# A selective scan fed by a conditioner: group loads two transfers a step, and two chains of small steps placed sooner on TensorE, ScalarE and VectorE

## The reference

```python
def _L0_cond_ref(x, ...):                      # the conditioner
    ctx = causal_ema(x, tau_ctx)
    wg = sigmoid(concat([x, ctx]) @ Wg.T + bg)
    gated = x * wg
    h1 = gelu(x @ Wn1.T + bn1)
    mod = 0.5 + sigmoid(h1 @ Wn2.T + bn2)      # one factor for each token and each of 8 traces
    traces = [causal_ema(gated * mod[d], tau[d]) for d in range(8)]
    temporal = sum(traces[d] * softmax(blend)[d] for d in range(8))
    gate = sigmoid(temporal @ Wtemp.T + btemp)
    soma = gelu(x @ Wsoma.T + bsoma)
    out = (soma * gate) @ Wout.T
    return (out - mean(out)) / sqrt(var(out) + 1e-5) * gamma + beta

def _L0_attn_ref(y, ...):                      # the mixer: a selective scan with 16 states, 512 channels
    xc, z = split(y @ W_in.T)
    xc = silu(causal_conv4(xc))
    dt, B, C = split(xc @ W_x.T)
    delta = softplus(dt @ W_dt.T + b_dt)
    for t: h = exp(delta[t] * A) * h + delta[t] * B[t] * xc[t];  y[t] = C[t] . h + D * xc[t]
    return (y * silu(z)) @ W_out.T
```

## Time and profile before

| | before |
|---|---|
| time, median of 3 runs | 3850.71 us (3850.57 to 3854.19) |
| the profiled execution | 3854.34 us |
| its span in the trace | 3852.6 us |
| granted TensorE clock, mean | 0.915 of full speed |
| busy: PE, DVE, ACT, POOL | 84%, 56%, 42%, 16% of the span |
| the stretch of the scans, 170 to 1640 us | DVE busy 1266.8 of 1470 us |

### The profile page before, as it was taken

The page is one execution under the profiler, slowest core; times in us unless marked ns, Lnnn a source line. Parts: engine busy times, 40 slices in busy tenths (PEclk is TensorE's granted clock), DMA queues, the critical chain, the costliest instruction groups (busy, mean ns, idle before and its releaser), DMA issues. The chain is left out here.

```text
span 3852.6 us, 40852 instructions
## 1 busy us (share of the span) xinstructions
PE 3246.7 (84%) x12812; PEld 1756.5 (46%) x12813; DVE 2152.1 (56%) x2705; ACT 1601.1 (42%) x3089; POOL 625.1 (16%) x767
## 2 busy tenths in 40 slices
PE   7677878787877864279979999999999999987996
PEld 5343434334343421046644444444444444445775
DVE  2398889888888888822223352535353444433334
ACT  3555555555656553123313242423333232322443
POOL 0000201020101010223310020201102020205772
PEclk8898989898888886589989999999999999998998
DMA  1345454636363646441230000000101010036557
GB/s 60 90 113 128 127 135 118 149 106 157 101 156 98 153 120 154 113 157 65 67 130 0 20 35 26 29 29 26 44 11 54 1 54 1 32 131 201 157 155 263
DMA packets 193227, 362.86 MB, mean 94 GB/s; under 512 B 28274, under 2 KB 85106, under 8 KB 191922
## 3 DMA queue, kind: packets, MB, share of 16 engines
q1 hardware_dynamic: 164514, 296.19, 27.2%
q0 software_dynamic: 20352, 57.17, 4.0%
q10 hardware_dynamic: 8208, 7.54, 0.6%
HBM read 250.53 MB, written 110.28 MB: 94 GB/s over the span
## 5 line engine op out<-in xcount | busy, mean ns | idle before, releaser
L1630 DVE TENSOR_TENSOR_SCAN hs<-dA,hs 128x2048 f32<-128x2048 f32 x128 | 566.2, 4423 | 7.0
L449 POOL COPY rows<-slot 128x64 f32<-128x64 f32 x48 | 13.4, 310 | 2796.1 <-DVE new_pl L586 2763.0
L2217 PE MATMUL ps<-pT,V 128*128 128x512 f32 x1024 | 450.7, 593 | 0.9 <-DVE pT L2385 0.9
L1471 ACT ACTIVATE dA<-dl,w_An 128x511 f32<-128x511 f32 x512 | 326.0, 711 | 204.7 <-DVE hs L1630 167.7
L1622 DVE TENSOR_TENSOR hs<-u,bb 128x2048 f32<-128x2048 f32 x128 | 292.6, 2286 | 108.7 <-DMA bb<-bcd 82.5
L1310 PE MATMUL ps<-hs,w_S 128*32 128x512 f32 x1024 | 170.2, 735 | 204.5 <-DVE hs L1636 204.5
L2217 PEld LDWEIGHTS ps<-pT,V 128*128 128x128 f32 x1024 | 189.6, 190 | 221.2 <-issue 214.8
L1636 DVE TENSOR_TENSOR hs<-hs,cb 128x2048 f32<-128x2048 f32 x128 | 289.9, 2266 | 0.0
L1787 POOL DMA_INDIRECT slots<-og,idt x232 | 242.4, 1045 | 260.4 <-DVE og L1875 197.2
L445 POOL DMA_INDIRECT sorted<-rows,new_pl x192 | 259.6, 1352 | 63.6 <-issue 44.8
L2292 ACT ACTIVATE pp<-ps,nm 128x512 f32<-128x512 f32 x256 | 172.6, 686 | 215.2 <-DVE nm L2368 215.2
(11 more groups left out here) (354 smaller groups left out, 5473.3 us busy)
## 6 DMA issues: line engine op xcount, KB each, us to landing
bb<-bcd SPq DMA_DIRECT2D x128, 256.0 KB
cb<-bcd SPq DMA_DIRECT2D x128, 256.0 KB
dl<-dld SPq DMA_DIRECT2D x128, 256.0 KB, 7.1
u<-ud SPq DMA_DIRECT2D x128, 256.0 KB, 9.3
xg<-sorted SPq DMA_DIRECT2D x232, 136.0 KB, 2.1
slots<-zeros SPq DMA_DIRECT2D x136, 128.0 KB, 3.8
qrg<-slots SPq DMA_DIRECT2D x32, 512.0 KB, 16.3
rg<-slots SPq DMA_DIRECT2D x32, 256.0 KB, 4.7
```

Source lines behind the costliest of these rows:

```text
L1471: act.activation(m.dA[:, N % 2, q, 1:T], m.dl[:, G % 2, q, 1:T], ACT.Exp, scale=An[:, e, N % GROUP:N % GROUP + 1]).then_inc(s_da, 1)
L1630: dve.tensor_tensor_scan(state, m.dA[:, N % 2].rearrange("p j t -> p (j t)"), state, 0.0, ALU.mult, ALU.add).then_inc(s_h, 1)
L2217: ins = pe.matmul(ps[:, 6 + j, :], V[:, m, h * D + j * P:h * D + (j + 1) * P], pT[:, i % 2, h % 2, m, :], start=(h == 0 and m == 0), stop= ...
```

## The change

1. **Group loads.** `spread_group` is split into `spread_delta` and `spread_u`. The first group of each subject is still brought in whole in step 14. Each of the other three is brought in over four steps, two transfers a step: delta in the first two, u in the last two. Before, the eight transfers stood in one step (3, 7 and 15).
2. **Conditioner, first pieces.** The product and the scaling of trace 0 of subject b + 2 move from step 0 of the next subject to step 15, `gate_product` over steps 13 and 14, and `gated_ready` from step 15 to step 14. `z_product` is cut in two halves between them.
3. **Conditioner, end.** ScalarE does `copy_ends` and `tempo_ready` ahead of the decays of step 7, and `cond_scale` ahead of those of step 9. TensorE does `cond_out_product` in step 8 and `variance_product` at the head of step 9. VectorE does `soma_gated` between `scan` and `out` of step 8, and `cond_ready` ahead of the gate of step 9.
4. **Delta.** TensorE does `rank_product` ahead of `mod_product` and `delta_product` already in step 12; ScalarE does `rank_ready` ahead of `mod_ready` and of the decays.
5. **Setup.** The table of decays is made from one copy of the identity in place of eight, after the first `gated_ready`; `setup_pe` runs in step 1 in place of 5, `setup_act` in step 4 in place of 5.

```diff
-        def spread_group(sp, m, G):
+        def spread_delta(sp, m, G, ns):
             j = G % JI
             sp.wait_ge(m_st if j else m_st0, 32 * (G // JI + 1))
             if G >= 2:
                 sp.wait_ge(s_da, GROUP * GROUP * (G - 1))
-            for n in range(GROUP):
+            for n in ns:
                 sp.dma_start(m.dl[LINE * n:LINE * (n + 1), G % 2], dld[j].rearrange("(q c) t -> c q t", c=LINE)
                              ).then_inc(s_dl[G % 2], 16)
...
@@ SyncE, in each step
-                            if n in (3, 7):
-                                spread_group(sp, m, JI * b + 2 + n // 4)
-                            if n == 15 and kc is not None:
-                                spread_group(sp, m, JI * kc + 1)
+                            G = (N + 1) // GROUP + 1
+                            if G % JI and 2 <= G < JI * B:
+                                piece = (N + 1) % GROUP
+                                spread = spread_delta if piece < 2 else spread_u
+                                spread(sp, m, G, range(piece % 2 * 2, piece % 2 * 2 + 2))
@@ ScalarE
                         elif n == 7:
-                            decays_ahead()
                             if kc is not None:
                                 copy_ends(act, c, kc)
                                 tempo_ready(act, c, kc)
+                            decays_ahead()
...
                         elif n == 9:
+                            if kc is not None:
+                                cond_scale(act, c, kc)
                             decays_ahead()
-                            if kc is not None:
-                                cond_scale(act, c, kc)
...
                             if kc is not None:
                                 conv_ready(act, m, kc, 3)
+                                rank_ready(act, c, kc)
                             if ke is not None:
                                 mod_ready(act, ke)
                             decays_ahead()
-                            if kc is not None:
-                                rank_ready(act, c, kc)
...
+                        else:
+                            if ke is not None:
+                                scale_turned(act, c, ke, 0, 0)
+                            if b >= 0 and kc is not None:
+                                decays(NS * kc)
+                            if ke is not None:
+                                scale_turned(act, c, ke, 0, 1)
                             decays_ahead()
@@ VectorE
+                            if n == 8 and b + 1 < B:
+                                soma_gated(dve, c, b + 1)
                             if N:
                                 out(N - 1)
...
                         elif n == 9:
+                            if kc is not None:
+                                cond_ready(dve, c, kc)
                             if b >= 0:
                                 gate(b, 1)
-                            if kc is not None:
-                                cond_ready(dve, c, kc)
...
-                        elif n == 15 and ke is not None:
+                        elif n == 14 and ke is not None:
                             gated_ready(dve, c, ke)
@@ VectorE, setup
+                ch.link(dve.tensor_copy(f.decay[:, :, :], ident[:, :].unsqueeze(1).to_broadcast([P, NTR, P])))
                 for d in range(NTR):
-                    ch.link(dve.tensor_copy(f.decay[:, d, :], ident[:, :]))
-                    ch.link(dve.tensor_tensor_scan(f.decay[:, d, :], ...
+                    ch.step(dve.tensor_tensor_scan(f.decay[:, d, :], ...
+                ch.all_but(0)
```

More of the change, by code:

```diff
@@ L301, in setup_dve @@
                 assert ch.n == f.averages, ch.n
-            elif part == 2:
+            elif part == 3:
                 ch.step(dve.tensor_copy(ones_b[:, :], ones[:, :]))
@@ L863, in delta_product, with z_product @@
                 product(pe, ps[:, 4 + j, :], [(Wdt[:, j * P:(j + 1) * P], c.dts)], m_dl)
-        def z_product(pe, k):
+        def z_product(pe, k, js):
             pe.wait_ge(m_pre, JI * (k + 1))
-            for j in range(JI):
+            for j in js:
                 product(pe, ps[:, 4 + j, :], [(Win[:, i, DI + j * P:DI + (j + 1) * P], y[:, i, :]) for i in range(DC)], m_z)
@@ L1250, in _ @@
                     for G in (0, 1):
-                        spread_group(sp, m, G)
+                        spread_delta(sp, m, G, range(GROUP))
+                        spread_u(sp, m, G, range(GROUP))
                     for b in range(B):
@@ L1335, in tasks @@
                             if kc is not None:
-                                turn_gated(pe, c, kc, 0, 0)
-                            if b > 0:
-                                add_state(NS * b - 1)
-                            if kc is not None:
-                                turn_gated(pe, c, kc, 0, 1)
+                                turn_gated(pe, c, kc, 1, 0)
                             if b >= 0:
@@ L1343, in tasks @@
                             if kc is not None:
-                                turn_gated(pe, c, kc, 1, 0)
+                                turn_gated(pe, c, kc, 1, 1)
+                            if b > 0:
+                                add_state(NS * b - 1)
                         elif n == 1:
@@ L1421, in tasks @@
                             convolution(pe, m, kc, 3)
+                            rank_product(pe, m, kc)
                             if ke is not None:
                                 mod_product(pe, c, ke)
-                            rank_product(pe, m, kc)
-                        elif n == 13 and kc is not None:
                             delta_product(pe, c, kc)
+                        elif n == 13 and ke is not None:
+                            gate_product(pe, c, ke, 0)
                         elif n == 14 and ke is not None:
-                            gate_product(pe, c, ke, 0)
                             gate_product(pe, c, ke, 1)
                         elif n == 15 and kc is not None:
-                            z_product(pe, kc)
+                            if ke is not None:
+                                turn_gated(pe, c, ke, 0, 0)
+                            z_product(pe, kc, (0, 1))
+                            if ke is not None:
+                                turn_gated(pe, c, ke, 0, 1)
+                            z_product(pe, kc, (2, 3))
                     pe.wait_ge(masks, MASKS)
@@ L1438, in _ @@
                     gate_product(pe, c, 0, 1)
-                    pe.wait_ge(f.su, f.averages)
+                    pe.wait_ge(f.su, f.mixed)
+                    turn_gated(pe, c, 0, 0, 0)
+                    turn_gated(pe, c, 0, 0, 1)
                     for n in range(NS):
-                        if n == 5:
+                        if n == 1:
                             setup_pe(pe, f)
+                            pe.wait_ge(f.su, f.averages)
                         if n == 8:
@@ L1455, in _ @@
                                 add_state(NS * b + n - 1)
-                            if n == 9 and kc is not None:
-                                variance_product(pe, c, kc)
                     add_state(last - 1)
@@ L1495, in tasks @@
                                 gate_of_z(b)
-                            if kc is not None:
-                                scale_turned(act, c, kc, 1, 0)
                         elif n == 1:
-                            if kc is not None:
-                                scale_turned(act, c, kc, 1, 1)
                             decays_ahead()
@@ L1599, in _ @@
                     gate_ready(act, c, 0, 1)
+                    scale_turned(act, c, 0, 0, 0)
+                    scale_turned(act, c, 0, 0, 1)
                     for n in range(NS):
-                        if n == 5:
+                        if n == 4:
                             setup_act(act, f, 1)
@@ L1663, in tasks @@
                                 route_choice(dve, v, rt, k)
-                        elif n == 8:
+                        elif n == 8 and k is not None:
+                            route_places(dve, v, rt, kc, k)
+                        elif n == 9:
                             if kc is not None:
-                                soma_gated(dve, c, kc)
-                            if k is not None:
-                                route_places(dve, v, rt, kc, k)
-                        elif n == 9:
+                                cond_ready(dve, c, kc)
                             if b >= 0:
                                 gate(b, 1)
-                            if kc is not None:
-                                cond_ready(dve, c, kc)
                         elif n == 11 and ke is not None:
```

45 lines of the change are left out of this document (26 added, 19 removed).

## The result

The changed kernel takes 3789.9 us (median of 4 runs, 3786.0 to 3794.2), the kernel before 3851.7 beside it: ratio 0.984, 95% interval 0.9828 to 0.9852, or 62 us less. The forecast was 3774, 76 us less; the range of 3718 to 3818 holds the result, and so does the own range of case (a).

The account below looks back on a forecast made before the run. VectorE's own work and waits set the scans' time, with 174 us of waits to win. Terms -50, +11, -40, +14, -8.5 and -2.7 sum to -76, taking 3850.7 to 3774 us; range 3718 to 3818.

Parts of the forecast that it names:

- case (a): Whole kernel: the terms add up as summed, 3774 us, own range 3750 to 3800; chance 0.45.
- the row of B: VectorE's waits for this row in the scans fall from 82.5 to 32.5 us with the group loads split: -50.
- y and delta: VectorE's wait at y goes, -40 us; its wait at L980 for delta grows from 6.0 to 8.0 in seven subjects, +14.
- u, taken as hidden: Last two u transfers of each split group land before `into` needs them: 7.7 us available, cost 0.
- rival (d): Halves of u come late at `into`, missing by 1.6 us in 23 groups: +37, 3811 us; chance 0.12.
- the wait in step 8: VectorE newly waits behind its scan for the temporal gate, 1.7 us in six subjects, 0.8 in the first: +11.
- setup and step 15: Setup: first `turn_gated` 2.9 us sooner, term -2.7; step 15: `gated_ready` fills the u wait, 9.7 to about 1, -8.5.
- (b): Row of B in time everywhere, no step 8 wait, L980 as before: -57 from the forecast, 3717 us; chance 0.17.
- (c): The 4 MB burst of step 14 alone decides and the row of B stays as late: 3824 us; chance 0.12.
- (f): Slower than before: late halves of u with a landing time of 12 us, +99, 3873 us; chance 0.06.
- (g): No change on balance, each wait removed comes back in the next step: 3851 us; chance 0.05.
- (e): ScalarE drains at each table switch ahead of `delta_parts`: +19, 3793 us; chance 0.03.

Follow-up runs that it names:

- Part 1 alone: The kernel before with only the group loads of the change, nothing else moved: 3825.8 us against 3857.4, ratio 0.9913.
- part 1 undone: The changed kernel with each group again brought in by eight transfers in one step: ratio 0.9941 to the kernel before.
- the early number: The changed kernel with the subject number brought in eight steps before it is read: 3776.0 us, ratio 0.9787 to the kernel before.
- u behind the row of B: The changed kernel with each pair of u transfers issued behind the row of B, not C; subject number as before: 3777.1 us, ratio 0.9799.
- the same with the early number: The changed kernel with pairs of u issued behind the row of B and the subject number brought in eight steps early: 3743.8 us, ratio 0.9728.
- the version with three edits: The changed kernel with early subject number, u behind the row of B, and TensorE's order rank, delta, then factor product: 3712.2 us, ratio 0.9645.

## Why the prediction was right, and where it was off

**Right: the row of B.** -50 predicted, -53.9 found, and what is left lies in step 2, mostly as said (the 0.8 us left for step 1 is not there). Part 1 alone and part 1 undone show that it brings the gain. That what is left in step 2 comes from the standstill for the subject number, which the prediction read from the earlier trace rows, is shown by the early number, 28.6 to 7.4. Whether megabytes at 206 GB/s are the right price of this row no run tells.

**Right: y and delta.** The wait at y went whole. Delta was forecast as +14: 37 us without part 4 and 19 for part 4. It is 34.4 and 16.7. The mechanism, that the cover of the rank product is gone, is shown by undoing it. The rule of the Trainium skill ("ScalarE: Activation LUTs", section "What ACT_TABLE_LOAD costs") of a drain of 1.38 us at each switch would, by an estimate from that figure for two switches, make the 5.55 us above 8.3. The trace does not agree: each of the two activations starts 0.02 us behind its table load of 1.28, and each table load 0.01 to 0.02 us behind the activation ahead of it.

**Off: u, taken as hidden.** This is the term that costs the forecast most: 0 predicted, +35.3 found. The step that failed is the 3.7 us for a pair, from 206 GB/s in the mean, against 7.7 us of time to its use. The 3.7 also counts the pair as 0.25 MB where it is 0.5; with that it would be 5.0 us and still inside the 7.7, so the slip alone does not explain the miss. The rate belongs to a stretch in which the DMA engines are full. The second of the pair of step 5 takes 9.8 us, and for the last 5.7 of them the engines are busy for 0.2 of their time at 67 to 105 GB/s (the last view of this document). In step 14, where eight transfers go out together, the last of the four of u lands after 10.0 us, no later. So for more than half of its time the pair did not fill the engines, and bandwidth was the wrong price; moving the zeros away changed nothing, while issuing the pair ahead of the row of C took the 33 us of waits of steps 3, 7 and 11 to 3.2. It was rival (d), +37, in size, but not in shape: it had 1.6 us in each of 23 groups, and the runs show 3.5 us in step 3 of seven subjects, where SyncE's issue is held for 4 us as well, 3.0 and 4.7 in step 7 of the first and the last subject, and at most 1.3 elsewhere. Why a single transfer takes some 5 us, and the second one 2 to 6 more, is open.

**Off: the wait in step 8.** Predicted +11, found 0. The prediction named this itself as a sign of being wrong: that the chain of steps 3 to 7 is paced by VectorE, so that step 8 has no wait. That came true. It let the chain of TensorE and ScalarE stand on its own. It does not: ScalarE's decays of step 6 stand between the two halves of the last trace's scaling, and they wait for VectorE's scan. The changed kernel, subject 1:

```profile
402.92 4.42 DVE L1644 TENSOR_TENSOR_SCAN hs<-dA,hs 128x2048 f32<-128x2048 f32 x1
407.44 2.56 ACT L1484 ACTIVATE dA<-dl,w_An 128x511 f32<-128x511 f32 x4 [2.19 <-DVE hs L1644]
409.90 0.81 ACT L907 ACTIVATE W0u<-ps,w_modT 128x256 f32<-128x256 f32 x2
...
423.23 0.69 ACT L922 ACTIVATE W0u<-ps,w_vec 128x512 f32<-128x512 f32 x1 [1.03 <-PE ps L410]
420.74 4.42 DVE L1644 TENSOR_TENSOR_SCAN hs<-dA,hs 128x2048 f32<-128x2048 f32 x1
```

The scan of step 6 ends at 407.34, the gate is ready 16.6 later at 423.92, and the scan of step 8 ends 17.8 later at 425.16. In subjects 1 to 6 of the changed kernel the gate is ready 16.6 us behind the scan of step 6, and VectorE comes 1.2 to 1.3 us after it. Counted from the end of step 2's residual, in us:

| kernel, subject | scan of step 6 ends | gate ready | scan of step 8 ends |
|---|---|---|---|
| changed kernel, 1 | 38.7 | 55.3 | 56.5 |
| part 1 undone, 1 | 36.0 | 55.3 | 53.9 |
| u behind the row of B, 2 | 36.4 | 55.6 | 54.2 |
| the same with the early number, 1 | 35.6 | 52.6 | 53.5 |

The predicted gate, 431.7, is 55.2 in this count, and that is what came. Where neither u nor the row of B of step 5 holds VectorE back (second and third row), its wait of 1.4 to 1.5 us is there, near the 1.7 forecast; in the other subjects of the third row's kernel it is 0.5 or less. In the changed kernel the late u of step 3 pushes VectorE behind the gate. So in that kernel a wait was replaced by another one ahead of it. With the late u gone as well, whether the wait appears depends on the chain's own length, 52.6 to 55.6; what lengthens it is told in the last section.

**Off: setup and step 15.** Setup gave nothing: the second gate of subject 0 was ready at 24.2 where I had 22.3, and `setup_pe` took 6.8 us of TensorE in its new place and 5.4 in its old one; the rest is in the spread named above. Step 15 kept 4.5 us where I had 1: 0.4 in each of the first four subjects, 0.6 to 1.3 in the other three, the last of which has no `gated_ready` to fill it.

**Luck.** The time lies 16 us from the forecast though the u term alone missed by 35. The wait of step 8 that did not come (11), delta (5), the row of B (4) and 6 us from unchanged code behind the mixers went the other way. The range was right for the sum; two of its terms, u and step 8, were wrong in mechanism.

**The rivals.** (b), (c), (f) and (g) are out as sums. (e) is not, 3793 lies 3 us from the result; it is out because its drain is not in the trace. (b)'s premise that the row of B clears everywhere needs the early number as well; the version with three edits reaches its time, 3714 against 3717.

## What to carry to other kernels

Price a small transfer by how long one like it takes from issue to landing in a quiet place, not by its bytes over the peak rate; when a burst is cut into pieces, each piece needs its whole landing time ahead of its use, and moving its issue ahead of a wait of the issuing engine can be worth more than removing bytes (here 23 us against none for 0.38 MB). Ask of each side chain which of its instructions stand behind one that waits for the engine it feeds: such a chain follows that engine, and a gain ahead of it is kept. Look at every round trip of the issuing engine (here a register loaded from memory, 11.6 us) as a stop for all that it issues.

## What the runs showed of the hardware

A wait of VectorE can cost TensorE its clock. With u behind the row of B, the first half of the subject product of step 3 (four matmuls) of subject 2 comes after 2.67 us in which TensorE waited for the residual, with only a skip term between, and runs at a granted clock of 0.50, 1.2 GHz. With the early number the same product comes after a gap of 0.58 us, at 1.00, which is 2.4 GHz. Rows of the timeline and a window, first of the kernel without the early number and then of the one with it:

```profile
544.24 2.07 PE L1337 MATMUL ps<-xs,w_Dg 128*128 128x512 f32 x2 [2.67 <-DVE xm L1666]
546.10 3.62 PE L410 MATMUL ps<-xm,ws 128*128 128x512 f32 x4
...
544.20:549.40 5.20, 5.16 (x6) 2.19 (x7) 5.20 (x2) 0.00 (x0) 0.00 (x0) 0.50 0.32 107
```

```profile
536.20 1.13 PE L1338 MATMUL ps<-xs,w_Dg 128*128 128x512 f32 x2 [0.58 <-DVE xm L1667]
537.16 1.88 PE L410 MATMUL ps<-xm,ws 128*128 128x512 f32 x4
...
535.00:540.00 5.00, 4.42 (x25) 2.37 (x18) 5.00 (x3) 3.69 (x7) 0.00 (x0) 1.00 0.32 119
```

The product takes 3.62 us in place of 1.88 and the skip term 2.07 in place of 1.13, on the chain that makes the temporal gate: 2.7 of the 3.0 us between 55.6 and 52.6 in the table above. With part 1 undone the product of subject 1 takes 3.62 us as well, and there too the gate is ready at 55.3. That this is the whole difference was not tried. It is not a rule either: in the changed kernel a gap of 2.81 us ahead of the same product of subject 1 left the clock at 1.00.

```profile
368.72 1.13 PE L1334 MATMUL ps<-xs,w_Dg 128*128 128x512 f32 x2 [2.81 <-DVE xm L1663]
369.68 1.88 PE L410 MATMUL ps<-xm,ws 128*128 128x512 f32 x4
```

The pair of u of step 5, issued at 397.1 and 397.5 with the rows of C and B and a piece of zeros next to it: the DMA engines' busy tenths and GB/s in 40 slices (0.35 us each) of the stretch from 396 to 410 us of the changed kernel:

```profile
DMA  2222228699999996222222222222222222221100
GB/s 88 99 105 94 102 97 164 257 351 222 181 164 170 161 170 155 105 94 94 105 105 94 94 99 99 105 79 67 76 76 79 97 105 94 105 82 47 47 35 0
```

For 20 slices (7 us) behind the one crowded piece the engines are two tenths busy at 67 to 105 GB/s, although the second transfer is under way until 407.3. The engines' peak is not what it waits for there; what is, no run shows.
